# Four graph layers in one program: context products in f16 halves, one masked turn, outer norms on ScalarE, and engine orders arranged anew

## The reference

```python
h = relu(layernorm(x)); x = x + block1(h, adj)     # layers 0, 1
h = relu(layernorm(x)); x = x + block2(h, adj)     # layers 2, 3
h = relu(layernorm(x)); x = x + block3(h, adj)     # layer 4, 12 heads, output matrix Wo
h = relu(layernorm(x)); x = x + block4(h, adj)     # layer 5, 12 heads
# layers 0 and 1
a = softmax(h @ h.T / sqrt(D)); delta = a * adj; attn = delta / (delta.sum(-1) + 1e-10)
ctx = (attn * upper) @ (h @ wl.T + bl) + diag(attn) * (h @ ws.T + bs) + (attn * lower) @ (h @ wr.T + br)
h = relu((ctx - mean) / sqrt(var + 1e-12) * g + beta)
# layers 2 and 3
u = u_left * upper(adj) + u_right * lower(adj)     # u_left = h @ (h @ W_left.T).T / sqrt(H), u_right alike
d = exp(u) * adj; ctx = d / (d.sum(-1) + 1e-10) @ (h @ W_lin.T + b_lin)
h = relu((ctx - mean) / (std + 1e-3) * a + b)
```

## Time and profile before

| what | value |
|---|---|
| time, median of 3 (lowest to highest) | 3185.84 us (3185.23 to 3186.56) |
| the profiled execution's own time | 3186.09 us |
| its span | 3184.3 us |
| busy time, PE / DVE / ACT / POOL | 3094.4 / 2685.0 / 1670.1 / 522.6 us |
| share of the chain that ended last | PE 95%, ACT 2%, DVE 1% |
| mean granted clock of TensorE | 0.99 |

### The profile page before, as it was taken

The page is one execution under the profiler, slowest core; times in us unless marked ns, Lnnn a source line. Parts: engine busy times, 40 slices in busy tenths (PEclk is TensorE's granted clock), DMA queues, the critical chain, the costliest instruction groups (busy, mean ns, idle before and its releaser), DMA issues.

```text
span 3184.3 us, 86264 instructions
## 1 busy us (share of the span) xinstructions
PE 3094.4 (97%) x34944; PEld 2411.7 (76%) x34944; DVE 2685.0 (84%) x7641; ACT 1670.1 (52%) x4437; POOL 522.6 (16%) x908
## 2 busy tenths in 40 slices
PE   4999999999999999999999999999999999999996
PEld 2777777777777777777777777777777777777774
DVE  5888888888888888888888888888888888888885
ACT  4455555555555555555555555555555555555553
POOL 1111111111111111111111111111111111111110
PEclk8999999999999999999999999999999999999997
DMA  5000000000000000000000000000000000000000
GB/s 172 11 8 13 9 11 13 8 13 13 8 13 13 7 13 14 7 13 13 8 13 13 7 13 13 7 13 10 11 13 8 13 13 8 13 13 8 13 7 6
DMA packets 37030, 47.73 MB, mean 15 GB/s; under 512 B 3679, under 2 KB 36635, under 8 KB 36635
## 3 DMA queue, kind: packets, MB, share of 16 engines
q1 hardware_dynamic: 30544, 33.31, 3.3%
q10 hardware_dynamic: 6090, 8.91, 0.9%
HBM read 29.59 MB, written 12.58 MB: 13 GB/s over the span
## 4 chain that ended last, share of the span: by engine, by line
PE 95%; ACT 2%; DVE 1%; issue 1%; POOL 0%; ACTq 0%; POOLq 0%
PE bank_a L270 27%; PE bank_c L270 23%; PE bank_b L270 20%; PE bank_c L314 7%; PE bank_b L301 4%; PE bank_c L444 4%; PE bank_b L308 2%; PE bank_b L314 2%; PE bank_c L460 1%; PE bank_c L461 1%; PE bank_c L459 1%; PE bank_a L347 1%; ACT htc_hi L565 1%; PE bank_b L397 1%; PE bank_a L314 1%
## 5 line engine op out<-in xcount | busy, mean ns | idle before, releaser
L579 ACT ACTIVATE prob<-score,neg_head_max 128x128 f32<-128x128 f32 x1536 | 489.0, 393 | 31.3 <-DVE neg_head_max L839 30.6
L270 PE MATMUL bank_c<-htc_hi,w_hi 128*128 128x128 f16 x2304 | 409.4, 219 | 0.0
L270 PE MATMUL bank_c<-htc_lo,w_hi 128*128 128x128 f16 x2304 | 409.3, 219 | 0.0
L270 PE MATMUL bank_c<-htc_hi,w_lo 128*128 128x128 f16 x2304 | 409.2, 219 | 0.0
L270 PE MATMUL bank_a<-w_hi,hta_hi 128*128 128x384 f16 x1152 | 377.4, 328 | 0.0
L270 PE MATMUL bank_a<-w_lo,hta_hi 128*128 128x384 f16 x1152 | 377.2, 328 | 0.0
L834 DVE SCALAR_TENSOR_TENSOR score<-bank_c,bias 128x384 f32<-128x384 f32 x512 | 280.0, 547 | 81.0 <-PE bank_c L444 80.8
L839 DVE TENSOR_REDUCE neg_head_max<-score 128x3 f32<-128x384 f32 x512 | 279.7, 546 | 8.9
L632 DVE SCALAR_TENSOR_TENSOR pt_lo<-bank_c,pt_hi 128x384 f16<-128x384 f32 x512 | 269.8, 545 | 2.2 <-ACT pt_hi L503 2.0
L936 POOL TENSOR_TENSOR rstd_b<-mean_var_b,plus_half 128x1 f32<-128x1 f32 x128 | 71.1, 555 | 1211.7 <-DVE mean_var_b L641 1211.7
L314 PE MATMUL bank_c<-ident,prob 128*128 128x128 f32 x1536 | 245.8, 276 | 9.5 <-ACT prob L579 9.3
(11 more groups left out here) (179 smaller groups left out, 8935.2 us busy)
## 6 DMA issues: line engine op xcount, KB each, us to landing
x_in<-x SPq DMA_DIRECT2D x64, 192.0 KB, 2.4
out<-y_out SPq DMA_DIRECT2D x64, 192.0 KB, 2.3
w_stage<-w_t ACTq DMA_DIRECT2D x8, 576.0 KB, 3.9
adj_in<-adj SPq DMA_DIRECT2D x64, 64.0 KB, 2.2
score<-w_t ACTq DMA_DIRECT2D x4, 576.0 KB, 3.8
prob<-w_t ACTq DMA_DIRECT2D x3, 576.0 KB, 4.0
norms<-norm_rows SPq DMA_DIRECT2D x8, 192.0 KB, 6.9
w_stage<-w_t SPq DMA_DIRECT2D x2, 576.0 KB, 5.4
```

Source lines behind the costliest of these rows:

```text
L270: mm = nc.tensor.matmul(out_ap, a, b, start=first and i == 0, stop=last and i == len(pairs_of) - 1)
L579: ex = nc.scalar.activation(prob[:, j, c, :], score[:, j, c, :], ACT.Exp, bias=neg_head_max[:, j, c:c + 1])
```

## The change

The diff does five things.

1. In layers 2 and 3, u and the context are computed from f16 halves, with m_hi and m_lo, lin_hi and lin_lo, attn_tb_hi and attn_tb_lo (hi by ACT, lo by DVE). htb_full is gone.
2. In layers 0 and 1, attn_a is one 128 column tile (the exponentials times adj). PE turns it once, and DVE multiplies the turned tile by the two triangles while it writes attn_ta. POOL's `mask_a` is gone.
3. The outer norms are done by ACT in two passes (a sum, then a sum of squares about the mean), with a scaling by `scale` and `shift`; DVE keeps two operations on one column each, POOL the power.
4. In layer 5 the biases of q and k are added by ACT when it copies q and k out of PSUM (three activations each with a bias column, loaded by six small DMAs of SP), instead of by matmuls. ACT makes bias2 instead of POOL.
5. ORDER, FIRST and SPLITS are new.

```diff
 ORDER = {
-    "pe": "xcxxyybayyyayyyxcbxwbwccwwcwccwcaccdacayyyyyyyyawcbwxxxxcxxxcwbcxcxwccbccabwcwyybaxxxx",
-    "act": "accbxccwpcpcpwpawccaccabcbcpbbpccpbpwxwbapbbwcbbcab",
-    "dve": "aaacbbabnabaaqaacccccbcbcbbcbpjpppjjjpjaaacaapaiaiimicainccbccczccpczbpbpbzbpaapbbbbpbapnp"
-           "nppbapaaca",
-    "pool": "lbaabcanqbm",
+    "pe": "yyybacbwwwwcwacwcbacxxcccxcxxxcxayybxxwwcabyybyyyyyydbwcwxxxxaxwcxcacxccwcccxbcxyyyyya",
+    "act": "ccxaqcbacwcwncppcpbpbwpbammmxbmcwibiiacniccbnjjjwcbcpccpppbwjncb",
+    "dve": "abcabccbcbcabccbcaapzppbpzazpabapabapaaaapbbpibxbcabibbiabbabcjbamcccjcccajaccbappppbapaaa"
+           "abncbbanqcpbax",
+    "pool": "qacmabbnab",
 }
 FIRST = {
-    "pe": {"a": (0, 4), "b": (1, 3), "c": (2, 10), "d": (1, 0), "w": (0, 6), "x": (1, 5), "y": (2, 8)},
-    "act": {"a": (0, 2), "b": (1, 1), "c": (2, 6), "p": (2, 4), "w": (0, 3), "x": (1, 1)},
-    "dve": {"a": (1, 15), "b": (2, 9), "c": (3, 9), "i": (2, 0), "j": (3, 0), "m": (2, 0), "n": (0, 1), "p": (3, 6), "q": (4, 0), "z": (3, 0)},
-    "pool": {"a": (1, 2), "b": (2, 1), "c": (3, 0), "l": (1, 0), "m": (1, 0), "n": (0, 0), "q": (2, 0)},
+    "pe": {"a": (0, 3), "b": (1, 6), "c": (2, 20), "d": (1, 0), "w": (0, 6), "x": (1, 9), "y": (2, 13)},
+    "act": {"a": (1, 2), "b": (2, 6), "c": (3, 15), "i": (2, 0), "j": (3, 0), "m": (4, 0), "n": (0, 1), "p": (4, 0), "q": (4, 0), "w": (1, 3), "x": (3, 0)},
+    "dve": {"a": (1, 13), "b": (2, 19), "c": (3, 18), "i": (2, 0), "j": (3, 0), "m": (2, 0), "n": (0, 0), "p": (4, 0), "q": (3, 0), "x": (2, 1), "z": (4, 0)},
+    "pool": {"a": (1, 2), "b": (2, 2), "c": (4, 0), "m": (2, 0), "n": (0, 0), "q": (3, 0)},
 }
 
 SPLITS = {
-    "act": [(0, 36), (0, 40), (0, 44), (0, 44), (0, 49), (1, 7), (1, 13), (1, 16),
-            (1, 19), (1, 19), (1, 22), (1, 23), (1, 28), (1, 29), (1, 36), (1, 40)],
-    "dve": [(1, 94), (1, 94), (1, 96), (2, 2), (2, 8), (2, 12), (2, 15), (2, 15),
-            (2, 40), (2, 47), (2, 54), (2, 59), (2, 59), (2, 59), (2, 73), (2, 78)],
+    "act": [(1, 39), (1, 48), (1, 48), (1, 61), (1, 61), (2, 3), (2, 7), (2, 9),
...
+    "dve": [(1, 59), (1, 64), (1, 79), (1, 87), (1, 92), (1, 97), (2, 0), (2, 17),
+            (2, 29), (2, 33), (2, 40), (2, 45), (2, 52), (2, 59), (2, 65), (2, 79)],
 }
...
+            for i in range(2):
+                m = W_INDEX[5] + i
+                for c in range(CHUNKS):
+                    sp.dma_start(qk_bias[:, i, c:c + 1], biases[m:m + 1, c * 128:(c + 1) * 128].rearrange("a p -> p a"))\
+                        .then_inc(qk_bias_loaded, 16)
...
                 cols = slice(o * 128, (o + 1) * 128)
-                ops = [(bias_hl[:, m, cols], ones2[:, :])] if biased else []
+                ops = []
...
-                    for i in range(2):
-                        mm = nc.tensor.transpose(a1[:, 128 * i:128 * (i + 1)], attn_a[:, i, :], ident[:, :])
-                    mm.then_inc(ata_done[g], 1)
+                    nc.tensor.transpose(a1[:, 0:128], attn_a[:, :], ident[:, :]).then_inc(ata_done[g], 1)
                     yield
                     pe.wait_ge(*attn_ta_ready.at(g, k))
-                    product(a1[:, 0:D], [(attn_ta[:, i, :], sides[:, i, :]) for i in range(2)]).then_inc(ctx_a_done[g], 1)
+                    product(a1[:, 0:D], [(attn_ta[:, 1 - i, :], sides[:, i, :]) for i in range(2)]).then_inc(ctx_a_done[g], 1)
...
-                    product(b1[:, 0:256], [(htb_full[:, c, :], m_sides[:, c, :, :]) for c in range(CHUNKS)])\
-                        .then_inc(ub_done[g], 1)
+                    ops = []
+                    for c in range(CHUNKS):
+                        ops += [(htb_hi[:, c, :], m_hi[:, c, :, :]), (htb_hi[:, c, :], m_lo[:, c, :, :]),
+                                (htb_lo[:, c, :], m_hi[:, c, :, :])]
+                    product(b1[:, 0:256], ops).then_inc(ub_done[g], 1)
...
-                    product(b0[:, 0:D], [(attn_tb[:, :], lin[:, :])]).then_inc(ctx_b_done[g], 1)
+                    product(b0[:, 0:D], [(attn_tb_hi[:, :], lin_hi[:, :]), (attn_tb_hi[:, :], lin_lo[:, :]),
+                                         (attn_tb_lo[:, :], lin_hi[:, :])]).then_inc(ctx_b_done[g], 1)
...
+            def scale(of, g, dst, src, done):
+                act.wait_ge(*root_ready[of].at(g))
+                act.wait_ge(*shift_ready[of].at(g))
+                nc.scalar.activation(dst[:, :], src[:, :], ACT.Identity, bias=shift[of][:, :], scale=rstd[of][:, :])\
+                    .then_inc(done[g], 1)
+
+            def moments(of, g, src, ready):
+                act.wait_ge(*ready)
+                nc.scalar.activation(spent[of][:, :], src[:, :], ACT.Copy, accum_out=total[of][:, :]).then_inc(total_ready[of][g], 1)
+                yield
+                act.wait_ge(*total_ready[of].at(g))
+                copy(neg_mean[of][:, :], total[of][:, :], scale=-1.0 / D).then_inc(neg_mean_ready[of][g], 1)
+                yield
+                act.wait_ge(*neg_mean_ready[of].at(g))
+                nc.scalar.activation(spent[of][:, :], src[:, :], ACT.Square, bias=neg_mean[of][:, :], accum_out=squares[of][:, :])\
+                    .then_inc(squares_ready[of][g], 1)
...
+            def middle_c(g):
+                yield from moments("c", g, x2[g % 2], x2_ready.at(g, 2))
+                scale("c", g, node_c[1], x2[g % 2], node_c_ready)
+                yield
...
-                    act.wait_ge(*ata_done.at(g, k))
-                    copy(attn_ta[:, :, :], chunked(a1[:, 0:256]), scale=1.0).then_inc(attn_ta_ready[g], 1)
-                    yield
...
-                    copy(m_sides[:, :, 0, :], chunked(b1[:, 0:D])).then_inc(ml_ready[g], 1)
+                    copy(m_hi[:, :, 0, :], chunked(b1[:, 0:D])).then_inc(ml_hi_ready[g], 1)
...
-                    copy(m_sides[:, :, 1, :], chunked(b0[:, 0:D])).then_inc(mr_ready[g], 1)
...
-                    copy(attn_tb[:, :], b1[:, 0:128], scale=1.0).then_inc(attn_tb_ready[g], 1)
+                    copy(attn_tb_hi[:, :], b1[:, 0:128], scale=1.0).then_inc(attn_tb_hi_ready[g], 1)
...
-                    copy(lin[:, :], b0[:, 0:D]).then_inc(lin_ready[g], 1)
+                    copy(lin_hi[:, :], b0[:, 0:D]).then_inc(lin_hi_ready[g], 1)
...
+                        else:
+                            if g == 0 and i == 0:
+                                act.wait_ge(qk_bias_loaded, 16 * 6)
+                            for c in range(CHUNKS):
+                                ins = nc.scalar.activation(qk[:, c, i, :], bank[:, c * 128:(c + 1) * 128], ACT.Identity,
+                                                           bias=qk_bias[:, i, c:c + 1], scale=INV_W)
+                            ins.then_inc(ready[g], 1)
...
+            def mask_c(g):
+                act.wait_ge(*adj_loaded.at(g))
+                if g:
+                    act.wait_ge(*score_ready.at(g - 1, QUADS))
+                copy(bias2[:, :], adj_in[g % 4][:, :], scale=2.0).then_inc(bias2_ready[g], 1)
+                yield
...
-            def outer_norm(of, g, src, dst):
-
-                yield from moments(of, g, 1, src)
-                add_eps(of, g, 1, 1e-5)
+            def outer_norm(of, g):
+
+                dve.wait_ge(*squares_ready[of].at(g))
+                V.tensor_scalar(var_eps[of][:, :], squares[of][:, :], 1.0 / D, 1e-5, ALU.mult, ALU.add)\
+                    .then_inc(var_eps_ready[of][g], 1)
                 yield
                 dve.wait_ge(*root_ready[of].at(g))
-                yield V.tensor_scalar(dst[:, :], src, mean_var[of][:, 0:1], rstd[of][:, :], ALU.subtract, ALU.mult)
+                V.tensor_tensor(shift[of][:, :], neg_mean[of][:, :], rstd[of][:, :], ALU.mult).then_inc(shift_ready[of][g], 1)
+                yield
...
-                    V.scalar_tensor_tensor(attn_a[:, :, :], expo_a[:, :].unsqueeze(1).to_broadcast([128, 2, 128]), 1.0,
-                                           adj_ul[:, :, :], op0=ALU.mult, op1=ALU.mult, accum_out=ul_sum[:, :])\
-                        .then_inc(attn_a_ready[g], 1)
-                    yield
-                    V.scalar_tensor_tensor(junk_a[:, :], expo_a[:, :], 1.0, adj_d[:, :], op0=ALU.mult, op1=ALU.mult,
+                    V.scalar_tensor_tensor(attn_a[:, :], expo_a[:, :], 1.0, adj_in[g % 4][:, :], op0=ALU.mult, op1=ALU.mult,
+                                           accum_out=edge_sum[:, :]).then_inc(attn_a_ready[g], 1)
+                    yield
+                    dve.wait_ge(*attn_a_ready.at(g, k))
+                    V.scalar_tensor_tensor(junk_a[:, :], attn_a[:, :], 1.0, ident[:, :], op0=ALU.mult, op1=ALU.mult,
                                            accum_out=d_sum[:, :]).then_inc(d_sum_ready[g], 1)
                     yield
-                    dve.wait_ge(*attn_a_ready.at(g, k))
-                    V.scalar_tensor_tensor(den0[:, :], z_sum[:, :], 1e-10, ul_sum[:, :], op0=ALU.mult, op1=ALU.add)\
-                        .then_inc(den0_ready[g], 1)
-                    dve.wait_ge(*d_sum_ready.at(g, k))
```

(37 more changed lines are left out.)

121 lines of the change are left out of this document (59 added, 62 removed).

## The result

The changed kernel takes 3137.53 us (median of 4 runs, 3135.49 to 3139.59) against 3185.53 for the kernel before beside it: ratio 0.9849, 95% interval [0.9837, 0.9862], 48 us faster. The forecast was 3111, with 3066 to 3160 as its range. So the sign and the range held, and the number was 26 us too good.

A forecast was written before the change was run, and what follows sets the result against it. PE's queue was taken as the bound: 48.17 us a graph less 1.5 and the old 0.4 hole, plus 0.6 of waits, gives 46.85; 157 + 63 x 46.85 - 2 + 2.9 = 3109.5 us span, 3111 us forecast, range 3066 to 3160.

The forecast's parts named there:

- PE's queue is the bound: Steady part: PE has no slack, so a graph gains what PE's queue gets shorter, less every new wait.
- What PE loses: Matmul work shortened or dropped in u, context, attn_a's turns and layer 5's bias: 1.5 us a graph.
- old hole of 0.4: PE's wait for htc_hi at layer 4's first value projection, 0.4 us a graph, counted as closed by the new order.
- The walk to layer 5's norm: Chain from Wo to node_c's turn ahead of layer 5: turn possible after 4.6 us, PE waits 0.4 us a graph.
- The lo halves: f16 low parts DVE writes ahead of PE's reads: two waits of 0.1 us, layer 1's context and layer 2's lin.
- DVE and ACT: Busy time of both engines stays below PE's: DVE near 2680 us, ACT near 2200 us.
- The fill: Time to the first y_out: 157 us instead of 153.9, with 41 us between node_b's and node_c's first turns.
- 1 us for the longer first norm: Graph 0's start: 1 us allowed in the fill because the first norm gets longer.
- Draining: End of the run: the last y_out starts 2 us ahead of the steady pace, instead of 7.0 before.
- Rival 1: The new order hides all waits: 46.25 us a graph, 3073 us; chance 0.22.
- Rival 2: Waits pile up at DVE's lo parts: 0.7 us a graph more, 47.55, 3155 us; chance 0.15.
- Rival 3: Square needs another ACT function table, so every norm reloads twice: 49.4 us a graph, 3272 us or more; chance 0.05.

The follow-up runs named there:

- e9: The kernel before, with all 19 weight matrices split before graph 0 starts instead of 3 before it and 16 between its stages: 3211.07 us.
- e10: The changed kernel, with all 19 weight matrices split before graph 0 starts: 3160.89 us.
- e12: Layer 5's norm moved back from ACT to DVE, against the changed kernel with its weight splits placed by need (3134.33 us): 3181.44 us.

## Why the prediction was right, and where it was wrong

**PE's queue is the bound: right.** Adding or taking work there moves the time by its pitches: 0.33 a graph for 0.33 of bias matmuls, 0.67 for 0.64 of u (this one with waits that came and went, as told above).

**What PE loses (1.5 us): right.** The pitch of 256 columns, in no row of before and taken as 0.109, is 0.108; u is 0.97 for 0.98. The old hole of 0.4 behind node_a's turn is gone, as argued. Period forecast 46.85, measured 46.955.

**The walk to layer 5's norm: right up to shift, short behind it and by one wait.** It put eps 2.6 us behind x2's start and shift at 3.4; the rows have 2.60 (1516.04 - 1513.44) and 3.40. But it let the scaling start at 3.6 and end at 4.3, and on ACT it is 3.91 and 4.62:

```profile
1516.87 0.31 ACT L602 ACTIVATE expo_b<-u_sum 128x128 f32<-128x128 f32 x1 [0.23 <-DVE u_sum L821]
1517.35 0.71 ACT L523 ACTIVATE node_c<-x,shift_c,rstd_c 128x384 f32<-128x384 f32 x1 [0.17 <-DVE shift_c L722]
```

expo_b runs to 3.74, and then ACT stands still for 0.17, because shift_c took 0.41 us and not 0.15 (more of this at the end). So the turn started 4.87 us after Wo (1518.11, against the three matmuls from 1512.75 and their pitches) instead of 4.6, and PE's holes on the way are 0.11, 0.23 and 0.29, together 0.63 for the 0.4. The 0.23 is the left product of the next graph's layer 1, which needs hta_lo. hta_lo was in the walk as work in DVE's way, but who waits for it was not asked. This stretch alone is 0.23 over the forecast, where the period is 0.105 too long; the rest of the period gave 0.12 back, which was not followed further.

**The lo halves: right in size, partly in place.** Two waits of 0.1 were forecast. The one of layer 1's context behind attn_ta does not come. Those at m_lo are 0.08 ahead of lin in layer 2 and the 0.11 ahead of u in layer 3, and both are gone in the kernel with u in f32; as idle time of PE m_lo shows once in the whole stretch from 250 to 2950 us, 0.3 us. The hole behind attn_b's turn at layer 5's start, 0.13, is a wait for ACT's htc_hi and not for a lo half.

**DVE and ACT: both a little lighter than forecast,** 2606 for 2680 and 2094 for 2200 us. Neither difference reaches PE. The single prices held within 0.04: two passes of 0.52 and 0.62 (0.48 and 0.575 taken), a read of 0.19, a scaling of 0.71 with two columns (0.67 taken), 0.36 for q and k with a bias column (0.28 to 0.37).

**The fill: wrong, and this is the failed step.** "That stretch took 64.9 to 103.1, 38 us. Now the 18.5 us of attention work of earlier graphs are missing from the 59, which leaves 41." It took 54.3. The step set a sum of PE work (59 - 18.5) beside a measured duration (38.2) of the kernel before. But of those 38.2 only some 27 are PE work by the pitches, and 11 are waits and pitches at the lower clock, in a string whose steady sum was 40: the missing attention work had been missing before too. Counted alike, the new stretch is 37 of work and at least those 11, 48 or more; measured were 37 and 17. And for all that stands ahead of it only "1 us for the longer first norm" was allowed, and 10.3 came. The first norm was not even longer (first turn at 19.7 for 19.9). With e9 and e10 the splits are excluded as a cause of the whole difference. Of the 7.7 us that this stretch grew there, 4.5 lie in layer 0, whose products stand in another order, and 3.2 in layer 1: 1.3 for the longer norm ahead of layer 2, 2 for the copy `sides` ahead of it on ACT. The order of layer 0's products and ACT's order were not looked at in the forecast. That layer 0's 4.5 come from the order of its products is read from the rows; no run changed that order alone.

**Draining: nearly right,** 3.6 us back for the 2 allowed.

**Rivals.** Rival 1 (46.25, 3073): the period excludes it. Rival 2 (waits pile up, 47.55, 3155): what PE waits for lo halves is 0.23 us a graph at hta_lo and 0.19 at m_lo, where the forecast had 0.2 and this rival 0.7 on top. With one norm more on DVE (e12) the period is 47.7. Rival 3 (a table load per norm): one load of 1283 ns in the run, with Square among Copy, Relu, Identity and Exp. By the Trainium skill, ScalarE: Activation LUTs, section "Table sets: the hidden batching unit", each switch of set would be paid anew; the trace has no switch.
